# Half-width row tiles, moving weights and a late shared expert in a ViT layer with a mixture of experts

## What is computed

```python
scores = jax.nn.sigmoid(x @ gate_weight.T)
sc = scores + gate_bias
grp = sc.reshape(T, N_GROUP, E // N_GROUP)
group_scores = jax.lax.top_k(grp, 2)[0].sum(-1)
_, gidx = jax.lax.top_k(group_scores, TOPK_GROUP)
...
_, topidx = jax.lax.top_k(masked, TOP_K)
tw = jnp.take_along_axis(scores, topidx, axis=-1)
tw = tw / (tw.sum(-1, keepdims=True) + 1e-20) * ROUTED_SCALE
g = jnp.einsum('th,ehi->tei', x, w_gate)
u = jnp.einsum('th,ehi->tei', x, w_up)
eo = jnp.einsum('tei,eih->teh', jax.nn.silu(g) * u, w_down)
cw = (jax.nn.one_hot(topidx, E, dtype=x.dtype) * tw[..., None]).sum(1)
routed = jnp.einsum('te,teh->th', cw, eo)
shared = jax.nn.silu(x @ shared_w_gate) * (x @ shared_w_up) @ shared_w_down
lg = topidx[:, 0] // (E // L)
...
out = routed + shared + ANCHOR_ALPHA * anchor
```

## Time and profile before

| | us |
|---|---|
| three runs | 420.84, 417.67, 415.27 |
| their median | 417.67 |
| profiled execution, span from the first to the last instruction | 412.1 |
| TensorE busy in the span | 343.3 (83%) |
| VectorE busy | 278.0 (67%) |
| ScalarE busy | 190.0 (46%) |
| POOL busy | 181.7 (44%) |

### The profile page before, as it was taken

How to read it: one execution, slowest core, us unless ns; L and a number is a source line. 1 busy time by engine, 2 the same in 40 slices (tenths; PEclk the granted TensorE clock), 3 DMA queues, 4 the chain that set the end, 5 groups by cost and what they waited for, 6 DMA issues and landing times.

```text
span 412.1 us, 8817 instructions
## 1 busy us (share of the span) xinstructions
PE 343.3 (83%) x2552; PEld 299.1 (73%) x2552; DVE 278.0 (67%) x1171; ACT 190.0 (46%) x471; POOL 181.7 (44%) x159
## 2 busy tenths in 40 slices
PE   5999999999899968773889999999999999994000
PEld 3786978779687857561677789999999999993000
DVE  0466789989798886798357775555565665666675
ACT  1152153441545233400157777777877777771000
POOL 6000000588888768767871374344422344433000
PEclk9999999999999997985989999999999999998555
DMA  7999999986698643694555576555555559531998
GB/s 234 298 335 335 329 341 328 420 320 119 123 337 252 126 96 86 218 387 137 152 162 130 167 214 180 162 158 165 165 145 162 166 155 291 168 113 58 303 303 245
DMA packets 55823, 88.44 MB, mean 215 GB/s; under 512 B 16145, under 2 KB 46521, under 8 KB 55513
## 3 DMA queue, kind: packets, MB, share of 16 engines
q1 hardware_dynamic: 38192, 67.66, 52.9%
q0 software_dynamic: 16720, 19.48, 17.8%
q10 hardware_dynamic: 864, 0.73, 0.6%
HBM read 50.62 MB, written 37.09 MB: 213 GB/s over the span
## 4 chain that ended last, share of the span: by engine, by line
PE 60%; DVE 20%; DMA 8%; issue 3%; ACT 3%; SPq 3%; DVEq 2%; POOLq 0%
PE B L823 20%; PE B L838 10%; PE B L514 6%; PE B L812 5%; DMA W<-sums_d 4%; PE B L549 4%; PE B L632 3%; PE B L598 2%; PE B L618 2%; DVEq L319 2%; DMA e_sb<-rows_d 2%; SPq L419 2%; DVE ring L1589 1%; PE B L656 1%; DMA W<-in_pt 1%
## 5 line engine op out<-in xcount | busy, mean ns | idle before, releaser
L457 POOL DMA_INDIRECT rows_d<-spent,slot x77 | 104.1, 1352 | 97.3 <-issue 90.9
L823 PEld LDWEIGHTS B<-e_sb,UPW 128*128 128x128 f32 x796 | 105.4, 193 | 10.7 <-issue 5.5
L823 PE MATMUL B<-e_sb,UPW 128*128 128x128 f32 x796 | 108.9, 278 | 1.5 <-issue 1.5
L1597 DVE TENSOR_TENSOR e_sb<-e_sb,B 128x128 f32<-128x128 f32 (+1 forms) x112 | 32.3, 288 | 62.2 <-ACT e_sb L990 55.8
L981 ACT COPY UPW<-W 128x512 f32 (+1 forms) x112 | 63.9, 570 | 22.2 <-issue 13.9
L838 PE MATMUL B<-W,e_sb 128*128 x224 | 69.3, 391 | 0.8 <-DVE e_sb L1597 0.8
L483 POOL DMA_INDIRECT sums_d<-spent x32 | 31.1, 972 | 48.7 <-DVE spent L1589 47.9
L812 PE MATMUL B<-ident,e_sb 128*128 128x128 f32 x224 | 43.1, 274 | 1.9 <-DMA e_sb<-rows_d 1.8
L990 ACT ACTIVATE e_sb<-B 128x128 f32<-128x128 f32 (+1 forms) x112 | 30.9, 276 | 22.2 <-PE B L823 20.8
L514 PE MATMUL B<-W 128*111 128x256 f32 (+1 forms) x132 | 34.2, 406 | 4.6 <-DMA W<-in_pt 4.5
L483 POOL DMA_INDIRECT sums_d<-W,tok_full x24 | 23.2, 966 | 30.3 <-ACT W L995 29.7
(11 more groups left out here) (250 smaller groups left out, 524.0 us busy)
## 6 DMA issues: line engine op xcount, KB each, us to landing
e_sb<-rows_d SPq DMA_DIRECT2D x112, 161.0 KB, 2.3
rows_d<-spent SPq DMA_DIRECT2D x2, 7728.0 KB, 44.4
W<-in_wx SPq DMA_DIRECT2D x1, 6643.0 KB
W<-sums_d SPq DMA_DIRECT2D x13, 448.0 KB, 9.4
W<-in_wx SPq DMA_DIRECT2D x10, 516.5 KB, 9.5
W<-in_wx SPq DMA_DIRECT2D x1, 4576.0 KB, 18.7
W<-in_pt SPq DMA_DIRECT2D x4, 666.0 KB, 6.9
W<-sums_d SPq DMA_DIRECT2D x7, 336.0 KB, 11.1
```

Of the source, the lines that this page charges most:

```text
L457: pool.indirect_dma_start(rows_d, bass.IndirectOffsetOnAxis(ap=slot[0:n, t, j:j + 1], axis=0), xrow[0:n, t, :], None).then_inc(done, 16)
L823: mm = pe.matmul(B[2 + i % 2][:, m * P:(m + 1) * P], UPW[:, i % 2, at:at + P], GT[:, i % 2, k, :], start=k == 0, stop=k == KC - 1)
L1597: dve.tensor_tensor(out[0:n, i % 2, :], S[0:n, i % 2, :], ups, ALU.mult).then_inc(H_ok, 1)
```

## The change

Each list's space in `rows_d` is 64 rows longer at its front and only 64 of its rows are zeroed. There are 88 tiles: 16 anchor tiles A and one a, then 32 pairs M F and 7 more F. An F or a tile is 128 rows of one list. An M or A tile is two halves of 64 rows: rows 0 to 63 are a full group of 64 of any list, rows 64 to 127 the last 64 rows of the list whose number is the tile's own, so its weights stand at a fixed place. SP loads the halves apart. The rows are stationary and the weights move, read from `W` in place: up is 2 matmuls of 256 columns (4 of half width in M; half as many columns for anchors), the hidden rows come out untransposed, are weighted with the product, transposed on TensorE, copied by ScalarE and multiplied with the down weights. No tile's result is added to another's: ScalarE copies each to one of seven buffers `Y`, POOL sends it. VectorE picks a row's weight and address by comparing codes. The table takes 27 VectorE instructions instead of 84 and holds two row addresses and one weight address per tile; TensorE reads four tiles' weight addresses at a time, SP two tiles' rows. The shared expert's blocks 3 to 5 stand behind the loop on TensorE, ScalarE and VectorE.

```diff
-LIST_ROWS = TOKENS
-DUMMY_ROW = P + LISTS * LIST_ROWS
+HALF = P // 2
+LIST_ROWS = TOKENS + HALF
+LAST_ROW = LISTS * LIST_ROWS + HALF - P
...
-ROWS_PACKED = -(-TOKENS * TOPK // P)
-LAST_FILLED = TOKENS * TOPK % P
-FULL = -(-(TOKENS * TOPK - EXPERTS * (P - 1)) // P)
-MIXED = ROWS_PACKED - FULL
-EXTRAS = EXPERTS - 1
-ANCHOR_PACKED = -(-TOKENS // P)
-ANCHOR_TILES = ANCHOR_PACKED + ANCHORS - 1
-KINDS = "A" * ANCHOR_TILES + "FFX" * 12 + "XM" * 6 + "XMM" * 13
+FULL_GROUPS = (TOKENS * TOPK - TOPK) // HALF
+FULL_ANCHORS = (TOKENS - 1) // HALF
+FULL = -(-(FULL_GROUPS - EXPERTS) // 2)
+KINDS = "A" * ANCHORS + "a" + "MF" * EXPERTS + "F" * (FULL - EXPERTS)
+ANCHOR_TILES = ANCHORS + 1
...
+FULL_AXIS, GROUP_AXIS = 1000, 2000
+GB, YB = 8, 7
...
+def tailed(i):
+
+    return KINDS[i] in "MA"
+
+
+def pieces(i):
+    return 2 if tailed(i) else 1
+
...
             of_choice = sums_d[1:1 + TP * OWN_ROWS, :].rearrange("(p c t) d -> p c t d", c=CHOICES, t=NT)
             n = TILES[-1]
             sp.dma_start(of_choice[n:TP, :, NT - 1, :], padrow[n:TP, 0:D].unsqueeze(1).to_broadcast([TP - n, CHOICES, D])).then_inc(ini_d, 16)
@@ -398,19 +415,19 @@
                 sp.dma_start(W[:, lo:hi], wx[:, lo:hi]).then_inc(ld["late1"], 16)
 
...
                     sp.wait_ge(T_ps, i - GB + 1)
-                    sp.wait_ge(meta_ok, i - GB + 1)
-                row = entry(mybir.EngineType.SP, 1, i, DUMMY_ROW + P)
-                sp.dma_start(G[:, i % GB, :], rows_d[bass.ds(row, P), :]).then_inc(g_ld[i % GB], 16)
+                    sp.wait_ge(pick_ok, i - GB + 1)
+                n = P // pieces(i)
+                for q in range(pieces(i)):
+                    sp.dma_start(G[q * n:(q + 1) * n, i % GB, :], rows_d[bass.ds(rows[q], n), :]).then_inc(g_ld[i % GB], 16)
...
+                    rows = entries(mybir.EngineType.SP, row_table[:, i:i + 2, :].rearrange("p i q -> p (i q)"), LAST_ROW)
+                load_rows(i, rows[i % 2 * 2:i % 2 * 2 + 2])
                 if i == XT - 16:
-                    sp.wait_ge(sent_anchor, 16 * ANCHOR_PACKED)
-                    sp.wait_ge(sent_full, 16 * FULL)
+                    sp.wait_ge(ini_d, 16 * 2)
+                    for k in range(YB):
+                        sp.wait_ge(sent[k], sent_until(k, ANCHOR_TILES))
                     load_part(TOPK)
             sp.wait_ge(D_ps, XT)
...
 
-            pool.wait_ge(hs_ok, NB)
-            pool.memset(spent[:, 0:until_scattered], 0.0).then_inc(mixed_zero, 1)
-            pool.wait_ge(scat_anchor, 16 * NT)
-            pool.wait_ge(scat, 16 * NT * TOPK)
-            pool.wait_ge(ini_d, 16 * 4)
...
-                pool.wait_ge(acc_ok, min(t + ANCHORS, ANCHOR_TILES))
-                if t == ANCHOR_PACKED - 1:
-                    pool.wait_ge(spared, 1)
-                send(ring_rows[:, t * RING + D:(t + 1) * RING], ring[:, t * RING:t * RING + D], sent_anchor)
-            for i in range(FIRST_ROUTED, XT):
-                k = INDEX[i]
-                if KINDS[i] == "F":
-                    pool.wait_ge(Y_ok, k + 1)
-                    send(tok_full[:, k:k + 1], Y[:, k, :], sent_full)
-                if KINDS[i] == "M":
-                    pool.wait_ge(acc_ok, sums_before(i) + 1)
-                    if k == MIXED - 1:
-                        pool.wait_ge(spared, 2)
-                    send(mixed_rows[:, k * RING + D:(k + 1) * RING], mixed[:, k * RING:k * RING + D], sent_mixed)
+            for i in range(XT):
+                pool.wait_ge(to_ok, i + 1)
+                pool.wait_ge(Y_ok, i + 1)
+                pool.indirect_dma_start(sums_d, bass.IndirectOffsetOnAxis(ap=to_row[:, i:i + 1], axis=0),
+                                        Y[:, i % YB, :], None).then_inc(sent[i % YB], 16)
 
...
                     fold()
-            shared_up(3)
-            stay_busy(5, 7, w_sgu)
+            stay_busy(8, 7, w_sgu)
             second_transposes(NB - 1)
             shared_down(2)
             route(NB - 1)
-            shared_up(4)
+            stay_busy(4, 7, w_sgu)
             rank(NB - 1)
-            stay_busy(12, 3, w_sgu)
+            stay_busy(8, 3, w_sgu)
             table_rows()
-            shared_down(3)
-            slot_bounds()
-            shared_up(5)
-            shared_down(4)
-            stay_busy(4, 3, w_sgu)
-            shared_down(5)
+            table_codes()
...
             def up(i):
 
-                pe.wait_ge(gt_by[copied_by_act(i)], copies_before(i) + 1)
-                pe.wait_ge(upw_ok, i + 1)
-                n = 2 if routed(i) else 1
-                for m in range(n):
-                    for k in range(KC):
-                        at = (k * n + m) * P
-                        mm = pe.matmul(B[2 + i % 2][:, m * P:(m + 1) * P], UPW[:, i % 2, at:at + P], GT[:, i % 2, k, :],
-                                       start=k == 0, stop=k == KC - 1)
-                mm.then_inc(U_ps, 1)
-
-            def down_weights(i):
-                size, at = (WX, UP_COLS) if routed(i) else (ANCHOR_WX, ANCHOR_UP_COLS)
-                e = entry(mybir.EngineType.PE, 0, i, (W_COLS if routed(i) else ANCHOR_COLS) - size)
-                return W[:, bass.ds(e, size)][:, at:at + D]
-
-            def down(i, weights):
                 if i == FIRST_ROUTED:
                     pe.wait_ge(ld["late0"], 16)
                     pe.wait_ge(ld["late1"], 16 * LATE_PIECES)
+                pe.wait_ge(gt_ok, i + 1)
+                n = 2 * (HIDDEN if routed(i) else ANCHOR_HIDDEN)
+                rows = P // pieces(i)
+                for k in range(KC):
+                    for q in range(pieces(i)):
+                        own = slice(q * rows, (q + 1) * rows)
+                        m = pe.matmul(B[2 + i % 2][own, 0:n], GT[:, i % 2, k, own], moved(i, q, k * n, n),
+                                      start=k == 0, stop=k == KC - 1)
+                m.then_inc(U_ps, 1)
+
+            def turn_hidden(i):
+
                 pe.wait_ge(H_ok, i + 1)
-                hid = H if routed(i) else H_anchor
-                pe.matmul(B[6 + i % 2][:, 0:D], hid[:, i % 2, :], weights, start=True, stop=True).then_inc(D_ps, 1)
+                pe.transpose(B[4 + i % 2][:, 0:P], H[:, i % 2, :], ident[:, :]).then_inc(HT_ps, 1)
+
+            def down(i):
+
+                pe.wait_ge(ht_ok, i + 1)
+                if i >= 2:
+                    pe.wait_ge(Y_ok, i - 1)
+                lo = UP_COLS if routed(i) else ANCHOR_UP_COLS
+                rows = P // pieces(i)
+                for q in range(pieces(i)):
+                    own = slice(q * rows, (q + 1) * rows)
+                    m = pe.matmul(B[6 + i % 2][own, 0:D], HT[:, i % 2, own], moved(i, q, lo, D), start=True, stop=True)
+                m.then_inc(D_ps, 1)
 
             turn_rows(0)
             turn_rows(1)
-            for i in range(XT):
-                if i >= 1:
-                    weights = down_weights(i - 1)
-                up(i)
+            load_offsets(0)
+            for i in range(XT + 2):
+                if i % PER_LOAD == PER_LOAD - 1 and i + 1 < XT:
+                    load_offsets(i + 1)
+                if i < XT:
+                    up(i)
+                if i >= 2:
+                    down(i - 2)
                 if i + 2 < XT:
                     turn_rows(i + 2)
-                if i >= 1:
-                    down(i - 1, weights)
-            down(XT - 1, down_weights(XT - 1))
+                if 1 <= i <= XT:
+                    turn_hidden(i - 1)
+            pe.wait_ge(Y_ok, XT)
+            shared_up(3)
+            shared_up(4)
+            shared_down(3)
+            shared_up(5)
+            shared_down(4)
+            shared_down(5)
...
-                shared_silu(b)
-
-            def copy_up(i):
-
-                size, n = (WX, UP_COLS) if routed(i) else (ANCHOR_WX, ANCHOR_UP_COLS)
-                e = entry(mybir.EngineType.Activation, 0, i, (W_COLS if routed(i) else ANCHOR_COLS) - size)
-                act.copy(UPW[:, i % 2, 0:n], W[:, bass.ds(e, size)][:, 0:n]).then_inc(upw_ok, 1)
-
-            def turned_copy(i):
-                act.wait_ge(T_ps, i + 1)
-                act.copy(GT[:, i % 2, :, :].rearrange("p k s -> p (k s)"), B[i % 2][:, 0:D]).then_inc(gt_by[True], 1)
 
             def hidden_silu(i):
                 n = HIDDEN if routed(i) else ANCHOR_HIDDEN
                 act.wait_ge(U_ps, i + 1)
-                act.activation(S[0:n, i % 2, :], B[2 + i % 2][0:n, 0:P], ACT.Silu).then_inc(silu_ok, 1)
-
-            def weigh(i):
+                if i >= 2:
+                    act.wait_ge(H_ok, i - 1)
+                act.activation(S[:, i % 2, 0:n], B[2 + i % 2][:, 0:n], ACT.Silu).then_inc(silu_ok, 1)
+
+            def keep_result(i):
                 act.wait_ge(D_ps, i + 1)
...
-                    copy_up(i + 2)
-                    if copied_by_act(i + 2):
-                        turned_copy(i + 2)
-                if i >= 1 and KINDS[i - 1] == "F":
-                    weigh(i - 1)
+                if i >= YB:
```

(64 more changed lines are left out.)

446 lines of the change are left out of this document (163 added, 283 removed).

## The result

The changed kernel takes 404.95 us (median of 4 runs, 403.52 to 410.82), the kernel before, beside it on the same chip, 417.65. The ratio is 0.967, 95% interval 0.960 to 0.973: faster by 12.7 us. The forecast was 395, a gain of 22.7 us. The profiled execution has a span of 401.7 us against 412.1. Of that execution the time is known too, 403.52, so 1.8 us lie around a span. If that holds before as well, most of the 5.6 that the forecast kept between the span of 412.1 and the median of 417.67 came of a quick execution under the profiler.

What follows compares the result with a forecast made beforehand. TensorE, busy throughout the routed loop, was taken as the bound, with a VectorE chain limiting the anchor stage before it. Span 412.1 - 23.5 (results earlier) + 1.1 (tail) = 389.7, plus 5.6 around it: 395 us; range 384 to 415.

Steps and rivals of the forecast that it cites:

- Start: Ahead of the anchor tiles: first up at about 198.5 us instead of 205.83, a gain of 7.3 us (up to 12).
- Routed tiles: Routed loop on TensorE: F 1.63 us, M 1.92 us, together 125.0 us against 133.7, a gain of 8.7 us.
- full overlap of the halves: M tile's up and down on TensorE: two 64-row halves run beside each other, otherwise 0.865 + 0.43 us more.
- 0.29 us for entering and leaving the form: TensorE in each tile of halves: one switch in ahead of up, one out ahead of the transposes; bounds 0 and 0.45.
- Rivals one: Up and down of M and A tiles on TensorE: halves do not overlap, 55 us more, 450 us; chance 0.05.
- two: Tiles of halves on TensorE: weight loads stand in the open, 1.1 us a tile, 54 us, 449 us; chance 0.04.
- rival three: From up to down in routed tiles: the new handoff between engines becomes the bound, F takes 1.93 us, 411 us; chance 0.13.
- Anchor tiles: Anchor stage ahead of the routed loop: 27.1 us instead of 34.7, a gain of 7.6 us, SP's loads hidden or nearly.
- the price of 1.50 us: An anchor tile in halves on TensorE: 4 x 0.111 + 0.43 + 0.22 + 0.11 + 0.29 us; 25.2 us in all.
- wait of tile 7 for the send of tile 0: Anchor stage, seven result buffers: tile 7 ready at 213.1 us waits until about 215 for POOL's send, 1.9 us.
- Drain and tail: Behind the loop: drain 2.3 us as before; shared expert beside the choices' return costs 0 to 3 us, taken as 1.1.
- Four: Result buffers and tail: sends land late behind scatters (4 us more), tail shows the full 3 us, 401 us; chance 0.08.

Runs made afterwards that it cites:

- e9: Changed kernel with ScalarE issuing eight half-tile loads, early silu table, shared expert ahead of the loop, 15 result buffers, late scatters held until the first tile's turn: 403.87 us.
- e2: Against the changed kernel, ScalarE instead of SP issues the second halves of the first eight anchor tiles: 401.40 us.

## Why the prediction came out as it did

*The whole.* The span came out 12.0 us above the forecast's 389.7: 5.4 ahead of the anchor scatter, which are a difference between executions, 4.7 in the anchor stage, 2.3 in the tail and 0.7 at the end of the loop, less 1.1 in the start. The second profile of after has 2.0, 4.8, 3.9, 0.7 and 0.5 in their place.

*Start: right.* Forecast were 19.4 us from the anchor scatter's issue to the first up, found 18.3 and 18.9. The late next was the scatter's landing, the first rows took 6.5 us to land (200.13 less 193.59; taken were 6.87 from the earlier trace rows), and TensorE's table read lay in the path.

*Routed tiles: right, to the term.* F 1.63 and M 1.92 us were forecast and measured; 32 pairs of 3.55 and 7 more F make the 125.0. So full overlap of the halves and 0.29 us for entering and leaving the form were the right readings; in the chain half of the 0.29 stands in M's up (1.01 against 0.86) and half in the transposes behind its down (0.37 against 0.22). The factor by which the 0.20 of the earlier trace rows became 0.29 was an estimate, and that it came out to the hundredth is luck. Rivals one, two and three fall: up in M is 1.01, not twice 0.86, the weight loads of the halves lie beside their matmuls, and no hole stands ahead of a down. The rule of the Trainium skill (TensorE: Matmul & The Clock Gate, section Part 3), by which weight loads with the same row group don't overlap a matmul, does not hold for these column halves, by the same 1.01 us.

*Anchor tiles: wrong, and of what the change touches most of the missing gain is here.* The first step that failed is "From 195.34 to 198.48 SP did two table loads and an issue; in such a time it now does one load and four issues, two tiles, so at most 1.57 a tile: hidden or nearly". Measured are 2.13 and 2.35 us a tile, against TensorE's 1.57. The figure was right for SP alone (1.50 with the scatters held back) and wrong beside them: I took three operations from the beginning of that stretch, and left out that the transfers which made the landing long make the issues long as well. By the chain it is this that sets the stage up to the tile turned at 220.02.

The second is the price of 1.50 us, which supposes the full clock. The first three steps took 8.1 us (202.85 to 210.97) instead of three times 1.50, but not by the rows alone: TensorE had stood idle for 2.41 and 1.60 us, and its granted clock was 0.50 until 210. With rows on time and the same clock they took 6.19 (scatters held back), with the clock at 1.00 as well 3.96 (e9). So of the 3.6 us too many some 1.9 would go with the rows on time, and 1.7 would stay with the clock, which in after hides behind the late rows. Two later waits cost 1.4, and the other 14 steps are 1.57 rather than 1.50, 1.0 in all; 0.6 are not assigned. That is why the ScalarE loads of e2, which took the row waits away, gave 2.5 us and still left 29.3 where 27.1 were forecast.

The forecast wait of tile 7 for the send of tile 0 (1.9) did not come, since the tile itself was late: POOL's first send went out at 214.36, and the up of tile 9 that stands ahead of that result started at 222.07. The mechanism exists: with the scatters held back it was the wait of 27.49 us.

*Drain and tail: right in kind, too small.* The drain took 3.0 us instead of 2.3: the downs of three tiles stand behind the last up where two stood before, and TensorE waits 0.61 us for ScalarE's copy ahead of the last two (at 360.14 and 361.56). The work behind the loop does hide beside the return, as said, and its place is worth nothing in the time (404.83 against 404.95); but the return itself ends 2.3 to 3.9 us later than forecast. Part of that is the spread between executions (the second profile of before is 2.3 us longer there as well); that some 1.8 us go with the work's place is a difference of medians of groups that touch, not shown. What the return waits for can be seen: the transfers themselves. Before (379 to 406 us) and after (366 to 396) the same 7.6 MB kept the 16 DMA engines busy for 95% of the time, at different rates:

```profile
DMA packets 2582, 7.68 MB, mean 284 GB/s; under 512 B 330, under 2 KB 534, under 8 KB 2582
q1 hardware_dynamic: 2534, 7.55, 94.9%
```

```profile
DMA packets 2561, 7.59 MB, mean 253 GB/s; under 512 B 319, under 2 KB 543, under 8 KB 2559
q1 hardware_dynamic: 2559, 7.57, 94.8%
```

The step that failed here is the count by VectorE's adds ("five choices at 3.3 us follow"): a choice came every 4.6 us, as the transfers brought it, and the adds of the last one began 31.7 us behind the results (362.7 to 394.33), where 27 to 31 were counted on. Why the rate differs, and how work that is done when the adds begin, at 369.67, could slow transfers that run to 394, was not found; the place of the results in memory is excluded.

*Rivals.* Four (401 us) came nearest in size. Its first half, sends late behind the scatters, is not what was seen: the rows were. Its second half, the tail, came: the adds end 35.0 us behind the last result (362.7 to 397.7), 31.6 before (34.0 in the second profile of before). The time lies above the forecast's own 386 to 404 us, and inside the wide range only because that reached into rival three, whose mechanism did not occur; that part is luck.

None of the variants is clearly faster than the change. What holds it is the stretch from the anchor scatter to the first routed tile, some 50 us in which 17 scatters and 33 row loads share the transfers and TensorE, idle ahead of the first rows, starts at half clock.

## To carry to other kernels

Price an issue from rows of the stage in which it will stand, with what else is in flight there, and take it from the whole stretch, not from its first three operations. When loads are cut in halves, count the issues: twice as many can turn a hidden queue into the one that is waited for. Moving a transfer ahead of another one gains only what the other has in slack, so look for who waits for that one before trying. And where a wait is removed, look for what it was hiding: here the granted clock of the first steps was the next limit.

## What was not expected of the hardware

The issue of a 64-row load takes longer than that of a 128-row load: in the loop of after 0.48 against 0.34 us (the second row below is the first half of an M tile, the first an F tile).

```profile
244.37 0.34 SPq L430 DMA_DIRECT2D G<-rows_d  x1
```

```profile
244.94 0.48 SPq L430 DMA_DIRECT2D G<-rows_d  x1
```

With indirect scatters of another queue in flight, SP's issues themselves grew long, not only their landings: 16 of them took 17 to 21 us against 12 with the scatters held back, while the scatters held their 1.65 us pace on POOL.
